# Linear attention regrouped from eight-token grids to 32 by 32 tiles of two tokens

## What is computed

```python
q = (xn @ wq + bq).reshape(b, n, H, HD).transpose(0, 2, 1, 3)      # H = 16 heads of HD = 16
k, v = ...                                                         # the same with wk, wv
fq, fk = elu(q) + 1, elu(k) + 1
kv    = einsum('bhnd,bhne->bnde', fk, v)        # per token: sum over the HEADS
qkv   = einsum('bhnd,bnde->bhne', fq, kv)
k_sum = fk.sum(axis=1)
qk    = einsum('bhnd,bnd->bhn', fq, k_sum)
attn  = (qkv / (qk[..., None] + 1e-6)) ... @ wo + bo
```

## Time and profile before

| | |
|---|---|
| runs | 728.37, 728.15, 726.8 us; median 728.15 |
| profiled execution, span from first to last instruction | 726.3 us |
| median of the runs less that span | 1.85 us |
| busy share of the span | PE 92%, DVE 66%, ACT 58%, POOL 45% |
| attention and MLP steps | about 172 to 556 us of the span |

### The profile page before, as it was taken

The page is one execution under the profiler, slowest core; times in us unless marked ns, Lnnn a source line. Parts: engine busy times, 40 slices in busy tenths (PEclk is TensorE's granted clock), DMA queues, the critical chain, the costliest instruction groups (busy, mean ns, idle before and its releaser), DMA issues.

```text
span 726.3 us, 17454 instructions
## 1 busy us (share of the span) xinstructions
PE 670.9 (92%) x6214; PEld 567.6 (78%) x6214; DVE 481.1 (66%) x1332; ACT 420.1 (58%) x841; POOL 326.5 (45%) x493
## 2 busy tenths in 40 slices
PE   7689999998777999999999999999999885999994
PEld 5449999975566788888888888888888663999994
DVE  7856757425688766767777768677676565777751
ACT  5755556502334767676767676766754642766660
POOL 5234563122232453545573664745547563353312
PEclk9879999999999999999999999999999998999998
DMA  8479788404656444544555555555433343567720
GB/s 264 149 241 322 229 270 276 139 29 119 98 99 109 91 66 90 95 87 66 101 86 85 117 84 129 68 108 91 86 73 96 116 132 109 167 215 217 219 93 29
DMA packets 287104, 95.56 MB, mean 132 GB/s; under 512 B 213989, under 2 KB 284737, under 8 KB 287019
## 3 DMA queue, kind: packets, MB, share of 16 engines
q1 hardware_dynamic: 272298, 85.48, 48.9%
q0 software_dynamic: 3840, 8.32, 3.6%
q10 hardware_dynamic: 10880, 0.66, 1.0%
HBM read 65.09 MB, written 29.40 MB: 130 GB/s over the span
## 4 chain that ended last, share of the span: by engine, by line
PE 75%; DVE 8%; issue 6%; ACT 4%; POOL 2%; DMA 2%; SPq 1%; ACTq 1%; POOLq 0%; DVEq 0%
PE bank L1735 68%; PE bank L1744 7%; DMA qkv_rows<-feats 1%; POOL hids L795 1%; SPq L373 1%; ACTq L373 1%; ACT hids L1038 1%; DMA x_all<-in_L_attn_q_x_dram 1%; ACT feats L1001 1%; POOL table L677 1%; ACT feats L999 0%; DVE kv_ L1679 0%; ACT ots L1063 0%; DVE sth L1687 0%; DVE att_ L1576 0%
## 5 line engine op out<-in xcount | busy, mean ns | idle before, releaser
L1735 PE MATMUL bank<-down_w,hids 128*128 128x256 f32 x768 | 105.8, 286 | 1.9 <-POOL hids L795 1.6
L1735 PE MATMUL bank<-hnts,up_w 128*128 128x512 f32 x384 | 104.4, 407 | 0.0
L795 POOL TENSOR_TENSOR hids<-hid,hids 128x512 fp32r<-128x512 f32 x64 | 83.1, 1298 | 41.0 <-ACT hids L1038 40.6
L1735 PEld LDWEIGHTS bank<-down_w,hids 128*128 128x128 f32 x768 | 95.7, 188 | 6.2 <-POOL hids L795 3.4
L1735 PE MATMUL bank<-qkv_w,xnts 128*128 128x256 f32 (+1 forms) x384 | 76.4, 346 | 5.7 <-DVE xnts L1589 4.8
L1735 PEld LDWEIGHTS bank<-hnts,up_w 128*128 128x128 f32 x384 | 67.5, 189 | 11.4
L1735 PEld LDWEIGHTS bank<-qkv_w,xnts 128*128 128x128 f32 x384 | 60.6, 189 | 18.2 <-DVE xnts L1589 7.5
L1035 ACT ACTIVATE hid<-bank,cols 128x512 f32<-128x512 f32 x64 | 44.1, 688 | 45.8 <-PE bank L1735 45.5
L786 POOL TENSOR_SCALAR sth<-sth 128x1 f32<-128x1 f32 x32 | 7.2, 226 | 125.3 <-DVE sth L1601 125.3
L1735 PE MATMUL bank<-a_w,xa_h 128*128 128x256 f32 x256 | 60.2, 379 | 0.0
L1735 PE MATMUL bank<-xa_xt,a_w 128*128 128x256 f32 x384 | 55.1, 294 | 1.4 <-DVE xa_xt L1327 1.4
(11 more groups left out here) (272 smaller groups left out, 1546.9 us busy)
## 6 DMA issues: line engine op xcount, KB each, us to landing
qkv_rows<-feats SPq DMA_DIRECT2D x32, 384.0 KB, 3.4
a_raw<-in_L_ffn_w_dram SPq DMA_DIRECT2D x32, 256.0 KB, 4.1
a_w<-in_L_ffn_w_dram SPq DMA_DIRECT2D x32, 256.0 KB, 3.7
b_raw<-in_L_ffn_w_dram SPq DMA_DIRECT2D x32, 256.0 KB, 3.2
b_w<-in_L_ffn_w_dram SPq DMA_DIRECT2D x32, 256.0 KB, 3.0
mid_rows<-x_all SPq DMA_DIRECT2D x8, 512.0 KB, 2.9
x<-mid_rows SPq DMA_DIRECT2D x32, 128.0 KB, 2.4
values<-qkv_rows SPq DMA_DIRECT2D x32, 128.0 KB, 2.9
```

Source lines behind the costliest of these rows:

```text
L795: pool.tensor_tensor(hids[1][u % 3][:], hid[u % 2][:], f32(hids[0][u % 3][:]), ALU.subtract).then_inc(s_hidl, 1)
L1735: return pe.matmul(dst, left, right, start=start, stop=stop, skip_group_check=True)
```

## The change

Two tokens take the place of eight in a grid. With `PAIR_TOKENS = 2` and `BANDS = 4` the 128 tokens of a tile are cut into four bands of 32 tokens; a band lies on 32 partitions (partition = 2 head + t), and a matmul contracts only the 32 partitions of its band.

- Each of `sum_kv` and `sum_att` is 64 float32 matmuls of 32 partitions x 32 columns against 32 columns, in place of 16 of 128 x 32 against 128. The four matmuls of one `g` stand on the diagonal of the array: band c of the rows and band c of the columns. All write to the same PSUM bank.
- `copy_kvt` on ACT and `turn_kv` on PE are gone. DVE reads `B_ATT` itself and transposes by 32 x 32 blocks to `kv_`, where it copied before.
- `feats` is stored by four transfers (one for each band) instead of one, into `qkv_rows` of the shape [3, T/4, 1024].
- Keys, values and queries are read by two transfers each (one for each token of a pair) instead of eight, one and eight. For the first seven tiles SP and ACT's queue issue one of each. SP issues keys ahead of values.
- `keys` and `queries` are a quarter as wide. Two unused tiles keep the SBUF addresses of what comes after, and one that was there before is gone.

```diff
-            engine.dma_start(keys[i][t * HEADS:(t + 1) * HEADS, :, t * HD:(t + 1) * HD],
-                             qkv_rows[1, rows, :].rearrange(
-                                 "(s t) (h d) -> t h s d", t=8, h=HEADS)[t]).then_inc(s_kvin[i], 16)
+            engine.dma_start(of_token(keys[i], t)[:, :, t * HD:(t + 1) * HD],
+                             band_rows(1, n).rearrange("(s t) (g d) -> t g s d", t=PAIR_TOKENS, d=HD)[t]).then_inc(
+                s_kvin[i], 16)
...
-                sp.dma_start(qkv_rows[:, rows, :].rearrange("c p d -> p c d"),
-                             feats[i][:].rearrange("p (c d) -> p c d", c=3)).then_inc(s_grid[i], 16)
+                for c in range(BANDS):
+                    store_band(sp, n, c)
...
-            def copy_kvt(n):
-                act.wait_ge(s_st1, n + 1)
-                if n >= 1:
-                    act.wait_ge(s_kvturn, n)
-                act.copy(kvt[:], bank[B_ATT][:].rearrange("p (i c) -> p i c", i=4)).then_inc(s_kvt, 1)
...
-                    dve.wait_ge(s_kvturn, n4 + 1)
+                    dve.wait_ge(s_st1, n4 + 1)
                     if n4 >= 1:
                         dve.wait_ge(s_st2, n4)
-                    dve.tensor_copy(kv[:], bank[B_KV][:].rearrange("p (i c) -> p i c", i=4)).then_inc(s_kv, 1)
+                    dve.transpose(kv[:], bank[B_ATT][:].rearrange("p (s t d) -> p s d t", s=SETS, t=PAIR_TOKENS)).then_inc(s_kv, 1)
...
-                for i in range(4):
-                    for j in range(4):
-                        last = mm(bank[B_ATT][32 * j:32 * j + 32, i * P:(i + 1) * P], values[n % 2][:, set_of(i, j)],
-                                  keys[n % 2][:, set_of(i, j)], True, True)
+                for g in range(SETS):
+                    for c in range(BANDS):
+                        band = slice(32 * c, 32 * c + 32)
+                        last = mm(bank[B_ATT][band, 32 * g:32 * g + 32], values[n % 2][band, g], keys[n % 2][band, g], True, True)
                 last.then_inc(s_st1, 1)
...
-            def turn_kv(n):
-                pe.wait_ge(s_kvt, n + 1)
-                for i in range(4):
-                    last = turn(bank[B_KV][:, i * P:(i + 1) * P], kvt[:, i])
-                last.then_inc(s_kvturn, 1)
```

More of the change, by code:

```diff
@@ L47, in build @@
     NOWHERE = 1 << 16
-    SETS = P // 8
+    PAIR_TOKENS, BANDS = 2, 4
+    SETS = P // (PAIR_TOKENS * BANDS)
     BATCH = 4 * GROUP
@@ L245, in build @@
         with ExitStack() as mid:
-            keys = tiles(mid, "keys_", 2, [P, SETS, P])
-            queries = tiles(mid, "queries_", 2, [P, SETS, P])
+            keys = tiles(mid, "keys_", 2, [P, SETS, 32])
+            queries = tiles(mid, "queries_", 2, [P, SETS, 32])
             values = tiles(mid, "values_", 2, [P, SETS, 32])
+            tile(mid, "weights_come_early", [P, 6 * KD * D * 2])
             feats = tiles(mid, "feats_", 2, [P, 3 * D])
-            kvt = tile(mid, "kvt_", [P, 4, P])
-            kv = tile(mid, "kv_", [P, 4, P])
+            kv = tile(mid, "kv_", [P, SETS, 32])
+            tile(mid, "weights_come_early_too", [P, KD * D])
             att = tile(mid, "att_", [P, HEADS, 32])
@@ L377, in issue_queries, with by_sp, store_band @@
-        def issue_queries(engine, n, t):
[L378 to L385, removed]
+        def by_sp(n):
+            return 1 if n < HELPED else PAIR_TOKENS
+        def store_band(engine, n, c):
+            i, q = n % 2, P // BANDS
+            engine.dma_start(qkv_rows[:, n * q:(n + 1) * q, c * D:(c + 1) * D].rearrange("i q d -> q i d"),
+                             feats[i][c * q:(c + 1) * q, :].rearrange("p (i d) -> p i d", i=3)).then_inc(s_grid[i], 16)
@@ L566, in load_keys @@
                     sp.wait_ge(s_st1, n - 1)
-                sp.dma_start(values[i][:, :, 0:HD], qkv_rows[2, rows, :].rearrange(
-                    "(s t) (g e) -> (t g) s e", t=8, g=HEADS)).then_inc(s_kvin[i], 16)
-                for t in range(keys_by_sp(n)):
+                for t in range(by_sp(n)):
                     issue_keys(sp, n, t)
+                for t in range(by_sp(n)):
+                    issue_values(sp, n, t)
             def load_queries(n):
@@ L574, in load_queries @@
                     sp.wait_ge(s_st2, n - 1)
-                for t in range(queries_by_sp(n)):
+                for t in range(by_sp(n)):
                     issue_queries(sp, n, t)
@@ L1055, in _ @@
                     logits_out_b(routed(s, 0), bank[B_V])
-                if at(s, 4) is not None and s != 4:
-                    copy_kvt(s - 4)
                 if at(s, 5) is not None:
@@ L1075, in _ @@
                     help_keys(1)
-                    copy_kvt(0)
                 if routed(s, 1) is not None and routed(s, 1) < NG - 2:
@@ L1575, in attended @@
                 dve.wait_ge(s_st2, n + 1)
-                dve.transpose(att[:], bank[B_ATT][:].rearrange("p (i t h) -> p h i t", i=4, t=8)).then_inc(s_att, 1)
+                dve.transpose(att[:], bank[B_ATT][:].rearrange("p (s t h) -> p h s t", s=SETS, t=PAIR_TOKENS)).then_inc(s_att, 1)
                 dve.wait_ge(s_att, step + 1)
@@ L2120, in _ @@
                     down_mid(g_down, 2 * j_down + 1)
-                if at(s, 4) is not None:
-                    if kv_free:
-                        pe.wait_ge(*kv_free)
-                    turn_kv(s - 4)
-                    kv_free = (s_kv, s - 3)
                 for n in turned_at(s, 0):
```

55 lines of the change are left out of this document (32 added, 23 removed).

## The result

The changed kernel takes **781.7 us** (median of 4 runs, 781.2 to 783.0) against 727.9 us for the kernel before (a fourth run of it added to the three above): ratio 1.074, 95% interval 1.072 to 1.076. I had forecast 718.4 us with a range up to 745, and "instruction supply" at 759 us for the case that a burst starves. It is slower than both.

What follows compares the result with a forecast made beforehand. PE's own list was taken to bound the steady stretch, chains between engines the first tiles. The span of 726.3 - 6.5 (steady steps) - 3.2 (first tiles) gave 716.6, plus 1.85 above the profiled span 718.4 us; range 708 to 745.

Steps and rivals of the forecast that it cites:

- instruction supply: Rival: PE's sequencer can't deliver a burst's 256 instructions as fast as the array takes them; 739 to 759 us, chance 0.12.
- the price of the burst: Time of 64 small matmuls in `sum_kv` or `sum_att`: taken as 1.10 us against 1.01 before, +0.09 a burst.
- lower end: Burst paced by the array, 32 groups 0.029 us apart: 1.04 us, +0.03 us a burst.
- upper end: Burst paced by issuing 256 instructions at 7 ns each: 1.9 us, +0.9 a burst, +34 us in 25 steps.
- given back: Rival: bursts near 1.2 us or another engine's chain takes up PE's gain; 725 to 730 us, chance 0.07.
- The second rival: "Instruction supply": PE's sequencer too slow for 256 instructions a burst, deciding from 1.23 us a burst; chance 0.12.
- serial bands: Rival: four row bands writing one bank run one after another, bursts of 3.83 us; near 875 us, chance 0.11.
- The rule of the Trainium skill: Cited against the bursts' arrangement: different row tiles can't access the same PSUM bank simultaneously; here all four write `B_ATT`.
- Transposes: PE's four transposes of `kvt_` go from each steady step: -0.44 us a step, 25 steps counted.
- Other engines: Steady stretch: ACT loses 32 copies, DVE's copy becomes a 0.704 us transpose, queues change; all beside PE, worth nothing.
- First tiles: Start of attention: shorter chain over `kvt_` -1.7 us, key issues and stores -1.5; sum -3.2, ends 0 and -7.
- The mechanism of the gain: PE's steady step loses 0.44 us of transposes for 2 x 0.09 of bursts: -0.26 us a step, -6.5 in 25.

Runs made afterwards that it cites:

- the wide variants: The two variants of the changed kernel with fewer, wider matmuls a burst, runs 1 and 2: 719.9 and 721.2 us.
- runs 1 and 2: Changed kernel with each burst as 16 matmuls of 128 columns, or 32 of 64 (wrong cross products): 719.9 us, ratio 0.987, and 721.2 us, 0.989.
- run 12: Changed kernel with its bursts on the upper 16 bits of the numbers, one pass, 128 instructions a burst, coarser products: 712.0 us, ratio 0.977.
- run 13: Kernel before the change with its bursts on the upper 16 bits, one pass, 32 instructions a burst, coarser products: 715.9 us, ratio 0.983.
- run 6: Changed kernel with the transfers of keys, values and queries cut to one of 16 sets, other data stale: 773.0 us, ratio 1.060.
- run 5: Changed kernel with each burst issued in two halves of 128 instructions, long matmuls between them: 780.7 us, ratio 1.072.
- run 7: Changed kernel's `sum_kv` on 32 by 32 tiles, in halves, the second after `qkv`; second sum of the kernel before, 16 matmuls: 756.9 us, ratio 1.036.
- 11: As run 7, but the second half of `sum_kv` stands ahead of the `qkv` products: 741.9 us, ratio 1.015.
- run 10: Kernel before with keys stationary and values moving in `sum_kv`, 16 matmuls on full tiles, no transposes by PE: 816.1 us, ratio 1.117.

## Why the prediction was wrong

**The step that failed is the price of the burst.** It was built from the issue rate and the array's rate within a burst: lower end 1.04 us, upper end 1.9, taken 1.10. Undisturbed it measured 1.22 us, inside the ends. With the transposes' 0.44 us gone that is -0.03 us a step, next to nothing, the case "given back". The average is 1.74 us (83.7 us by 48), since the upper end was bounded by how fast PE issues what it has, not by how fast it gets it. The second rival had the right word, supply, and the wrong place and price: it decided from 1.23 us a burst, and the kernel lost 35 us there with bursts of 1.22. What decides is the time between two ends of blocks of 256 instructions, and I had not priced the instruction queue at all, though the page of before shows its 50 packets. The loss of 34.9 us in the steady stretch is near the +34 of my upper end by accident. The prediction also had no term for the clock, which took about 6 us of it.

The Trainium skill has the mechanism: "Runtime: NRT & Kernel Launch", section Instruction fetch mechanics, says that PE's instruction memory is refilled in 16 KiB blocks of 256 instructions while the present one runs, and that crossing a block is mostly hidden. The block size agrees with the trace (1.59 MB in 97 packets). That it is hidden holds for the kernel before, with 11.3 us a block and no distance over 0.12 us at a block's end from 172 to 600 us, and not here, with bursts that use one up in 1.2 us.

The other steps:
- **No serial bands.** Right. All four row bands write one bank side by side: 32 groups of four in 1.07 us are 0.033 us a group (I had 0.029). The rule of the Trainium skill against it, cited in the prediction, isn't borne out.
- **Transposes.** -0.44 us a step was right; 10.2 us in 24 steps (the prediction counted 25, but 295 us hold 24 steps of 12.25), and the wide variants kept 8.6 and 7.8 of it.
- **Other engines.** DVE's transpose from `sum_kv` takes 0.706 us and hid as said; in the steady stretch the queues cost nothing.
- **First tiles.** -3.2 us was wrong twice. Stops at blocks' ends took 10.7 us there, and the clock was at its lower level for part of it. But without stops the wide variants show +0.6 us as well: the issues of 64-byte rows cost 0.66 us where I had assumed 0.39 from transfers of another shape, and the wait for `kvt_` was replaced by one for the queries.
- **The mechanism of the gain** stands: without the dense bursts the change is worth 4 to 9 us, as runs 1 and 2 (9.2 and 8.0 us) and run 12 against run 13 (3.9) show.

## What to carry over

Count instructions, not only microseconds. Where a change multiplies the instructions of one engine, take from the profile how long 256 of them last, where they are densest, and how long a fetched block takes to become usable (here 4 to 5 us from one block to the next); a pass that costs the array nothing may still cost a block. Splitting many small matmuls over a step helps only if the parts don't meet other traffic, and each part pays for its own start and end.

## What the runs showed of the hardware that I had not expected

- PE stops at the end of a block of 256 instructions that lasted too short: at 15 of 20 ends with under 3.2 us of work, 5 of 26 with 3.2 to 5, 1 of 33 with more. It goes on 1.2 to 1.7 us after the 16.4 KB packet has ended. Halving the DMA share left this as it was (run 6).
- Away from the blocks' ends too, dense bursts can get only a few instructions every 0.65 to 0.7 us, in a place of the step where GpSimd issues indirect transfers (all eight such places in run 5 and in run 7, gone in 11). What in that place does it is open, and so is how the two kinds of stop hang together.
- The granted clock fell to the 1.2 GHz level at the end of four of the 14 long stops at blocks' ends between tiles 7 and 31 or within 1.1 us after it, which cost about 6 us on top of the stops. In run 10 it fell without a stop in a burst.
- Small float32 matmuls on separate column bands follow each other at 4.2 ns an instruction, and a tile of 32 rows costs the same as one of 128 rows (1.22 and 1.23 us a burst). Stationary columns count as moving ones do, 0.11 us per 128.
